# Two attention layers in one kernel: softmax sums out of the value products, division a step later, projections two steps ahead, and three of eight bias additions on GpSimd

## The reference

```
xn = layernorm(x)                                  # layer 0
s  = softmax(q k / sqrt(8) + bias[h]) v  @ w_out   # 16 heads of 8, bias from relative position
g  = silu(top-2-of-8 experts(xn))
x  = x + s * g
xn = layernorm(x)                                  # layer 1
a  = resid * softmax(causal(q k / sqrt(8))) + skip * eye - centre * uniform
x  = x + (a v @ cproj) * silu(xn W + xn V C + b)
```

## Time and profile before

| what | us |
|---|---|
| median of 3 runs | 1045.06 (1040.49 to 1049.14) |
| span of the profiled execution, first to last instruction | 1042.1 |
| setup, to the first projection | 0 to 76 |
| first layer's attention | 76 to 489 |
| experts and middle | 489 to 733 |
| second layer's attention | 733 to 1042 |

### The profile page before, as it was taken

The page is one execution under the profiler, slowest core; times in us unless marked ns, Lnnn a source line. Parts: engine busy times, 40 slices in busy tenths (PEclk is TensorE's granted clock), DMA queues, the critical chain, the costliest instruction groups (busy, mean ns, idle before and its releaser), DMA issues.

```text
span 1042.1 us, 22685 instructions
## 1 busy us (share of the span) xinstructions
PE 867.5 (83%) x7795; PEld 551.3 (53%) x7814; DVE 728.4 (70%) x1177; ACT 456.1 (44%) x808; POOL 393.3 (38%) x421
## 2 busy tenths in 40 slices
PE   1884887999999999987999998525689999999986
PEld 0742443555555555544555555314467667676763
DVE  5564686999899999985665555365456767676763
ACT  1251333545444554533433333258354445454532
POOL 7007772111111111100577776673134334344432
PEclk9996788999999999997999999856899999999998
DMA  4797441332223333204122122240544453435320
GB/s 135 232 142 173 111 113 44 82 75 62 62 63 74 76 81 72 61 7 140 37 59 53 54 56 56 69 125 16 118 98 89 98 103 97 103 97 103 97 44 11
DMA packets 105527, 88.21 MB, mean 85 GB/s; under 512 B 12565, under 2 KB 97497, under 8 KB 102409
## 3 DMA queue, kind: packets, MB, share of 16 engines
q1 hardware_dynamic: 96780, 76.54, 32.4%
q0 software_dynamic: 4352, 8.99, 2.8%
q10 hardware_dynamic: 4352, 2.10, 0.9%
HBM read 45.69 MB, written 41.11 MB: 83 GB/s over the span
## 4 chain that ended last, share of the span: by engine, by line
PE 19%; issue 14%; POOL 8%; DMA 5%; ACT 3%; DVE 3%; SPq 1%; POOLq 0%; ACTq 0%; DVEq 0%
PE ps L666 7%; POOL probs L1137 5%; PE ps L687 3%; DMA ks<-parts_d 3%; PE ps L678 2%; PE ps L660 2%; POOL qkr L1124 1%; ACT rows L888 1%; PE ps L668 1%; POOL qk L1129 1%; DMA parts_d<-qk 1%; PE ps L1469 1%; DVE mx L1191 1%; PE ps L1411 1%; DMA probs<-mixed 0%
## 5 line engine op out<-in xcount | busy, mean ns | idle before, releaser
L1191 DVE TENSOR_REDUCE mx<-ps 128x4 f32<-128x1024 f32 (+1 forms) x224 | 269.5, 1217 | 106.2 <-PE ps L1411 68.4
L1338 ACT ACTIVATE probs<-probs 128x1024 f32<-128x1024 f32 x128 | 135.3, 1057 | 165.6 <-DVE probs L1201 163.1
L1201 DVE TENSOR_TENSOR probs<-ps,tabB 128x1024 f32<-128x1024 f32 x128 | 152.4, 1212 | 3.6 <-PE ps L1431 3.6
L1343 ACT ACTIVATE probs<-ps 128x1024 f32<-128x1024 f32 x96 | 96.5, 1024 | 96.3 <-PE ps L1469 38.6
L1460 PE MATMUL ps<-probs,vpad 128*32 128x256 f32 (+1 forms) x2048 | 132.5, 365 | 3.0 <-ACT probs L1338 1.1
L1137 POOL TENSOR_TENSOR probs<-probs 128x512 f32<-128x512 f32 x64 | 78.9, 1264 | 136.7 <-PE ps L1460 136.7
L1403 PE MATMUL ps<-tabA,eyeb 128*128 128x512 bf16 x256 | 101.9, 398 | 31.2 <-DVE probs L1201 18.0
L1405 PE MATMUL ps<-ks,qs 96*128 96x256 bf16 x512 | 101.7, 281 | 0.0
L1431 PE MATMUL ps<-qs,ks 99*128 99x256 bf16 x512 | 76.7, 279 | 11.1 <-DVE mx L1191 6.0
L666 PE MATMUL ps<-qs,probs 128*128 x144 | 81.7, 650 | 1.4
L1460 PE MATMUL ps<-probs,onespad 128*32 128x256 f32 x1024 | 82.3, 394 | 0.0
(11 more groups left out here) (227 smaller groups left out, 1593.1 us busy)
## 6 DMA issues: line engine op xcount, KB each, us to landing
parts_d<-qk SPq DMA_DIRECT2D x64, 192.0 KB, 2.3
qs<-parts_d SPq DMA_DIRECT2D x32, 384.0 KB, 4.9
ks<-parts_d SPq DMA_DIRECT2D x32, 384.0 KB, 6.7
parts_d<-qk SPq DMA_DIRECT2D x64, 128.0 KB, 1.9
slots_in<-probs SPq DMA_DIRECT2D x1, 4680.0 KB
probs<-slots_in SPq DMA_DIRECT2D x72, 65.0 KB, 1.8
parts_d<-qk SPq DMA_DIRECT2D x64, 64.0 KB, 1.6
probs<-mixed SPq DMA_DIRECT2D x16, 256.0 KB, 3.3
```

The lines of the kernel that those rows point to most:

```text
L1191: nc.vector.tensor_reduce(mx[:, s.buf(), t, heads[0]:heads[-1] + 1], ring[:, slot].rearrange("p (h n) -> p h n", n=w), AX.X, ALU.max).then ...
L1201: nc.vector.tensor_tensor(probs[:, j, :].rearrange("p (h n) -> p h n", n=T), ring[:, slot].rearrange("p (h n) -> p h n", n=T), v.tabB[:, h ...
L1338: nc.scalar.activation(probs[:, j, :], probs[:, j, :], ACT.Exp).then_inc(exp_done, 1)
L1343: nc.scalar.activation(probs[:, j, :], ring[:, slot], ACT.Exp).then_inc(exp_done, 1)
```

## The change

What it does: (1) `vpad` gets eight columns of ones beside each head's eight values, so that one value product gives outputs and sums in one bank; `onespad`, the ones products, `sums` and `add_tiles` go. (2) `divide` goes. ScalarE copies the bank out, SP sends it to DRAM, reads the sums back as 128 by 32, VectorE inverts these, SP sends the inverses out and reads them back spread over eight partitions, and VectorE multiplies a step later (`scale`). Output projection, `add_shape`, `project` and store move from batch k-2 to k-3. (3) The projections and parts are for batch k+2 instead of k+1, and the stacks of k+1 are loaded at the start of SP's step. (4) In the first layer, from step 3 on, ScalarE copies B tiles 0, 2 and 4 out of PSUM (`take`), GpSimd adds their bias in place (`bias_aside`), and ScalarE takes their exponential two tiles later. The order of value products is changed to fit; the experts' weights are loaded from ScalarE's queue; the loop has three rounds and more steps are unrolled.

```diff
-        v.vpad = sb("vpad", [P, 3, 8, 160])
-        v.onespad = sb("onespad", [P, 4, 32])
+        v.vpad = sb("vpad", [P, 3, 8, 128])
+        v.od_d = nc.dram_tensor("od_d", (8, 2, 16, T), F32, kind="Internal")
+        v.rec_d = nc.dram_tensor("rec_d", (H, T), F32, kind="Internal")
...
+            nc.gpsimd.memset(v.vpad[:].rearrange("p b c (i w) -> p (b c i) w", w=32)[:, :, HD:2 * HD], 1.0
+                             ).then_inc(zeroed, 1)
...
-    LATE = 2 if layer else 6
-    PROJECT = 10 if layer else 11
-    LOOP = 3
+    LATE = 2 if layer else 4
+    SCALE = 2 if layer else 0
+    INVERT = 7 if layer else 10
+    VALUES = {9: (0, 1)} if layer else {13: (0, 1), 15: (2, 3)}
+    ASIDE = () if layer else (0, 2, 4)
+    ORDER = tuple(range(NU)) if layer else (1, 0, 3, 2, 5, 6, 4, 7)
+    PROJECT = 10 if layer else 8
+    LOOP, HELP = 4, 3
-    LAG = {"QK": 1, "V": 0, "E": -2, "Y": -2, "M": 0}
+    LAG = {"QK": 2, "V": 0, "E": -3, "Y": -3, "M": 0}
...
+            def parts(s, c):
+                b = s.buf(2)
+                (done,) = ahead(s.n(2) + 1)
+                sp.wait_ge((s1_done, s2_done, s3_done)[c], done)
+                for a in range(2):
+                    sp.dma_start(v.parts_d[b, a, PART_ROWS[a][c]].rearrange("r p t -> p r t"), ...).then_inc(part_st, 16)
+            def outputs_out(s):
...
+                sp.wait_ge(ev_done, done)
+                for r in range(2):
+                    sp.dma_start(v.od_d[:, r].rearrange("k d t -> k (d t)"), ev[:, r, :]).then_inc(od_st, 16)
+            def sums_in(s):
...
+                sp.wait_ge(od_st, stored)
+                sp.dma_start(rec[:], bass.AP(v.od_d, HD * T, [[16 * T, H], [2 * H, HD], [1, 2 * H]])).then_inc(sum_ld, 16)
+            def outputs_in(s):
...
+                sp.dma_start(raw[:], v.od_d[:].rearrange("k r d t -> (k r) d t")[:, 0:HD]).then_inc(raw_ld, 16)
+            def inverses_out(s):
...
+                sp.wait_ge(rd_done, done)
+                sp.dma_start(v.rec_d[:, :].rearrange("h (e t) -> (h e) t", e=HD), rec[:]).then_inc(rec_st, 16)
+            def inverses_in(s):
...
+                sp.wait_ge(rec_st, written)
+                sp.dma_start(rden[:], v.rec_d[:, :].unsqueeze(1).broadcast_to([H, HD, T])).then_inc(rec_ld, 16)
...
+            def body(s):          # SP; each under its own s.has(...)
+                stacks(s); parts(s, 0); outputs_out(s); parts(s, 1); sums_in(s); outputs_in(s)
+                parts(s, 2); inverses_out(s); inverses_in(s); maxima(s)
...
+        def bias_aside(pool, s, n, j):
+            pool.wait_ge(taken, len(ASIDE) * (s.n() - HELP) + n + 1)
+            p = probs[:, j, :].rearrange("p (h n) -> p h n", n=T)
+            nc.gpsimd.tensor_tensor(p, p, v.tabB[:, heads[0]:heads[0] + 4, off:off + T], ALU.add).then_inc(biased, 1)
...
             def body(s):          # GpSimd
-                if layer and s.has(-2):
-                    for g in range(GROUPS):
-                        add_tiles(pool, s, g)
+                for n, j in enumerate(apart(s.k)):
+                    if n == 1 and s.has(2):
+                        rest_two(pool, nc.gpsimd, s)
+                    if s.has(-1):
+                        bias_aside(pool, s, n, j)
...
-            def divide(s):
+            def invert(s):
+                dve.wait_ge(sum_ld, 16 * (s.n(-2) + 1))
+                nc.vector.reciprocal(rec[:], rec[:]).then_inc(rd_done, 1)
+            def scale(s):
+                dve.wait_ge(raw_ld, 16 * (s.n(-3) + 1))
+                dve.wait_ge(rec_ld, 16 * (s.n(-3) + 1))
+                nc.vector.tensor_tensor(on[:], raw[:], rden[:], ALU.mult).then_inc(on_done, 1)
...
+            def take(s, j, slot):
+                act.wait_ge(full["B"], NU * s.n(-1) + j + 1)
+                nc.scalar.activation(probs[:, j, :], ring[:, slot], ACT.Copy).then_inc(taken, 1)
+            def outputs(s):
+                act.wait_ge(pv_done, NU * (s.n(-2) + 1))
+                nc.scalar.activation(ev[:].rearrange("p r t -> p (r t)"), od, ACT.Copy).then_inc(ev_done, 1)
...
                 for pos, (kind, j) in enumerate(U.order):          # ScalarE
+                    if pos == (0 if layer else 4) and s.has(-2):
+                        outputs(s)
                     if kind == "B" and U.exists(s.k, kind):
-                        exponential(s, j, U.slot(s.k, pos))
+                        if j in apart(s.k):
+                            take(s, j, U.slot(s.k, pos))
+                        else:
+                            exponential(s, j, U.slot(s.k, pos))
+                        if apart(s.k) and j in (2, 4, 6):
+                            exponential(s, j - 2, 0)
...
-                for what in range(2 if layer == 0 else 1):
-                    for n, h in enumerate(heads):
-                        lhs = vpad[:, b, 4 * c + q, 32 * i:32 * i + 32] if what == 0 else onespad[:, i, :]
+                for n, h in enumerate(heads):
+                    at = 32 * i - 16 * (i // 2)
+                    mm = nc.tensor.matmul(od[32 * q:32 * q + 32, T * (i % 2) + t0:T * (i % 2) + T],
+                                          vpad[:, b, 4 * c + q, at:at + 32], probs[:, j, w * n:w * n + w], ...)
-            def sums(s, g):
...
                 for pos, (kind, j) in enumerate(U.order):          # TensorE
-                    if layer == 0 and pos == 1:
-                        last_values()
-                    if pos == 1 and s.has(1) and s.k != 0:
+                    if layer == 0 and pos in (1, 3):
+                        late_values(pos + 3, pos + 5)
+                    if pos == 1 and s.has(2):
                         projections(s)
```

More of the change, by code:

```diff
@@ L1056, in heads_of, with apart, freed, ready @@
         return range(8 * (j - 4), 8 * (j - 4) + 8), (0 if kind == "A" else 1), P
+    def apart(k):
+        return ASIDE if k >= HELP else ()
+    def freed(s, d, j):
+        m, aside = s.n(d), apart(s.k + d)
+        if not aside:
+            return used["B"], NU * (m - 1) + j + 1
+        if j in aside:
+            return taken, len(aside) * (m - HELP) + aside.index(j) + 1
+        before = sum(i not in aside for i in range(j))
+        return used["B"], NU * (HELP - 1) + (NU - len(aside)) * (m - HELP) + before + 1
+    def ready(s, d, j):
+        return NU * (s.n(d) - 1) + (ORDER.index(j) if apart(s.k + d) else j) + 1
     def emit(eng, body):
-        pipeline(eng, body, 0 if layer else -1, LOOP, 4, B + 1, 3, B)
+        pipeline(eng, body, -1 if layer else -2, LOOP, 3, B + 2, 3, B)
     with nc.Block() as block:
@@ L1070, in stacks @@
                 b = s.buf(1)
-                first, second, third, stored, scored = ahead(
-                    s.n(1) + 1, s.n(1) + 1, s.n(1) + 1, 16 * PART_DMAS * (s.turn(1) + 1), NU * (s.n(-2) + 1))
-                for c, made, wait in ((0, s1_done, first), (1, s2_done, second), (2, s3_done, third)):
-                    sp.wait_ge(made, wait)
-                    for a in range(2):
-                        rows = PART_ROWS[a][c]
-                        sp.dma_start(v.parts_d[b, a, rows].rearrange("r p t -> p r t"),
-                                     qk3[:, a, c, :].unsqueeze(1).broadcast_to([P, PARTS - c, T])
-                                     ).then_inc(part_st[b], 16)
-                sp.wait_ge(part_st[b], stored)
+                stored, scored = ahead(16 * PART_DMAS * (s.n(1) + 1), NU * (s.n(-2) + 1))
+                sp.wait_ge(part_st, stored)
                 if s.has(-2):
@@ L1097, in body @@
                     stacks(s)
+                if s.has(2):
+                    parts(s, 0)
+                if s.has(-2):
+                    outputs_out(s)
+                if s.has(2):
+                    parts(s, 1)
+                if s.has(-2):
+                    sums_in(s)
+                    outputs_in(s)
+                if s.has(2):
+                    parts(s, 2)
+                if s.has(-2):
+                    inverses_out(s)
+                    inverses_in(s)
                 if s.has():
@@ L1102, in _ @@
                 ahead_of[0](sp)
-                body(first)
+                for c in range(PARTS):
+                    parts(first, c)
                 sp.wait_ge(v.cleared, 4)
@@ L1264, in project @@
                     nc.vector.tensor_tensor(y, xt, y, ALU.add).then_inc(fin_done, 1)
             def body(s):
-                if layer == 0 and s.k == 0:
-                    rest_one(dve, nc.vector, s)
-                    rest_two(dve, nc.vector, s)
                 for pos, (kind, j) in enumerate(U.order):
-                    if layer == 0 and pos == 1 and s.has(-2):
-                        divide(s)
+                    if pos == SCALE and s.has(-3):
+                        scale(s)
                     if U.exists(s.k, kind):
-                        (maximum if kind == "A" else add_bias if layer == 0 else lambda *a: None)(s, j, U.slot(s.k, pos))
-                    if kind == "A" and j == NU - 1 and s.has() and (layer or s.k < LOOP):
```

(13 more changed lines are left out.)

219 lines of the change are left out of this document (113 added, 106 removed).

## The result

The changed kernel takes 1001.93 us (median; 998.65 to 1002.62) beside 1042.78 us of the kernel before in the same comparison: ratio 0.9584, 95% interval 0.9542 to 0.9626. Forecast 989, range 961 to 1030. Its profiled execution has a span of 999.9 us. ScalarE's copy of the transposed maxima marks the end of each step in both traces (106.18, 135.12, ... before; 110.43, 136.31, ...

What follows compares the result with a forecast made beforehand. VectorE was taken to bound the first layer's loop, TensorE the second's. First layer -7, -38, +5.5 and second -3, -15.5, +2 make -56 from 1042.1, to 986; the median 3.0 above gives 989, range 961 to 1030.

Steps and rivals of the forecast that it cites:

- First layer's step: First attention loop: a chain through last exponential, maxima's copy, projections and score tiles gives 19.9 us, 2.9 us less a step.
- Rival (b): First layer: GpSimd's additions take 4 us instead of 2.5, copies and exponentials queue behind, 1 us a step, 1002; chance 0.05.
- signs of being wrong: Reciprocals waiting for DMA in the first layer, low clock in the loops, ScalarE waiting for GpSimd.
- Start: First layer's start: 7 us less, from the 6.00 us scatter wait and 1 us of ones products on a slow clock.
- End of the first layer: Last exponential to last output: four landings of about 2 us, +7.5; the last step gives 2 back, +5.5 in all.
- Second layer's step: Second attention loop: SP's ordered transfers close the step before TensorE does, at 16.3 us, 1.2 us less a step.
- SP's chain: SP's ordered queue: stacks' loads, stores, outputs out, then sums in, for VectorE's reciprocal; sets second-layer steps at 16.3 us.
- Rival (a): Second layer isn't held by SP's queue and goes at TensorE's 15.1 us a step: another 15.5 less, 973; chance 0.12.
- The lock: VectorE's new product and GpSimd block each other in SBUF: 0.4 us a step at most, some 10 us in all.
- End of the second layer: The end grows from 12.7 us to about 16, +4, and the last step gives 2 back: +2.
- rival c: TensorE's clock falls in first-layer steps: half its path slow, 1024, chance 0.11; whole path slow, 1059, chance 0.03.
- rival d: SP's transfers from outputs out to sums in land later than priced; decides from 2.3 us extra, at 3.5 about 1080; chance 0.07.

Runs made afterwards that it cites:

- no_aside: Changed kernel with part 4 undone: VectorE adds all eight biases, ScalarE makes no copies, GpSimd adds none; 1017.58 us.
- rows_early: Changed kernel with ScalarE copying the first layer's transposed maxima out before its last exponential instead of after it; 994.25 us.
- take_first: Changed kernel with ScalarE copying first-layer tile 4 out for GpSimd before tile 3's exponential instead of after it; 998.12 us.
- all_edits: Changed kernel with both second-layer edits, earlier weights, earlier tile 4 and maxima copies, GpSimd's help from step 4, and tile 4's exponential before tiles 5 and 6; 964.85 us.
- weights_early: Changed kernel with the experts' weight loads issued behind tile 2's exponential in the first layer's last step instead of behind the last exponential; 995.13 us.
- scale_first: Changed kernel with the second layer's VectorE product of outputs and inverses moved to the start of the step; 995.07 us.
- both edits: Changed kernel with the second layer's product moved to the step's start and SP issuing the outputs' stores before the first part's stores; 988.00 us.
- parts_vector: Changed kernel with the first layer's maxima's parts made by VectorE behind its last maximum instead of by GpSimd; 1049.16 us.
- outputs_first: Changed kernel with SP issuing the second layer's two output stores ahead of the first part's two stores; 996.63 us.
- help_later: Changed kernel with GpSimd beginning to help in the first layer in step 4 instead of step 3; 996.14 us.

## Why the prediction was right, and which term was off

- **First layer's step: right.** 19.92 us over twelve steps (20.05 without the first and the last two), 19.9 forecast; the two idle stretches of VectorE are there, a third before tile 0 costs nothing in the sum. The same chain gave 21.3 for no_aside, measured 21.37. Its last link was too simple: the last exponential's copy, value tile 4 behind its exponential, and the parts behind GpSimd's third addition all reach the projections within about 0.5 us. Taking away one (rows_early, take_first) shows nearly nothing; the third had to go too (all_edits).
- **Parts' costs: right.** GpSimd's addition 2.37 us (2.5 taken), ScalarE's copies 1.01 and 0.59, reciprocal 0.35, product 0.41. The first layer's reciprocals wait for no DMA in a full step. Rival (b) is off. Of the forecast's signs of being wrong one came, in a single step: in step 3 ScalarE waits for GpSimd.
- **Start: near in the sum (-7.4 for -9.9) by luck.** "A step later the scattering is over" held for VectorE's output. The forecast left out that GpSimd itself, which part 4 needs in that very step, comes free no sooner. Steps 1 and 2 gained 13.5 us where 7 were forecast, step 3 lost 1.8 instead of gaining 2.9, and the setup lost 4.2, which lies within its spread.
- **End of the first layer: the mis-sized term, +13.7 for +5.5.** From the last exponential to the last output it was +15.0 for +7.5. The forecast put the weights "beside" this chain and priced its landings at 2 us; the first took 8.3, and in a steady step 3.9. weights_early shows that the weights did that, for 3.5 us against the changed kernel and 2.5 against the best run with the loads in their place. Of the rest, the last value products ran at almost half speed (3.58 us for 1.93, clock 0.53 for 1.00), after TensorE had stood 2.38 us. The last step's -2 was -1.3.
- **Second layer's step: near in size (16.55 for 16.3), half right in cause.** SP's chain exists and has the size forecast (16.42 in scale_first), but the reciprocal waited for it in few steps, since VectorE was as late by the product held up beside GpSimd. Rival (a), TensorE's 15.1, needs both limits away; with both edits 15.86 was reached.
- **The lock: cost wrongly bounded.** The forecast gave the rule of the Trainium skill (SBUF — State Buffer, section "Who interferes with whom") 0.4 us a step at most, the product's own length. By that rule, in my words, the one that comes second is blocked for the whole instruction of the other; the trace agrees: what counts is GpSimd's 1.16 us (product 1.29 for 0.48, second layer) or what was left of its 2.37 us (pass 1.98 for 0.18, parts_vector). In the first layer the product isn't held up (0.41 us). The price could be read before the change: in the middle part of the kernel before, a VectorE product of 128x512 took 1.73 us beside GpSimd's additions and 0.68 beside a GpSimd fill, and GpSimd's own addition 1.72 instead of 1.26. Timelines of VectorE and GpSimd before:

```profile
681.54 1.73 DVE L832 TENSOR_TENSOR probs<-probs,rows 128x512 f32<-128x512 f32 x1 [13.62 <-POOL probs L821]
...
691.18 0.68 DVE L832 TENSOR_TENSOR probs<-probs,rows 128x512 f32<-128x512 f32 x1
...
682.68 1.72 POOL L821 TENSOR_TENSOR probs<-probs 128x512 f32<-128x512 f32 x1
```

- **End of the second layer: -0.2 for +2.** From the last exponential (981.33) to the last result 16.3 us, +3.5 for +4; the last step gained 3.8 instead of 2. In the eight other runs with the second layer untouched this whole stretch takes 29.8 to 32.0 us, so 2 us can't be told here.
- **Clock (rival c): not in the changed kernel's loops (1.00).** One edit away it is there: in parts_vector TensorE waits 2.11 us in each step, and 1.4 us of slow products follow. With it the kernel is no faster than before.
- **Slower (rival d): off.** In the steps SP's chain never cost the extra 2.3 us from which it decides; only at the first layer's end did a landing take that much more.
- **The 13 us between 989 and 1001.93:** 8.2 are the first layer's end, 3.4 the second layer's thirteen steps, 2.5 the start with step 3, 2.2 the experts and the middle; the rest gives some 3.5 back.

## What to carry to other kernels

Some VectorE passes that work in SBUF alone (here a product of two SBUF tiles and a cast of 128x32) cost what is left of the GpSimd pass beside them, so look for a place in the step where GpSimd is idle before trusting their usual duration. Not all do: the bias additions, with one operand in PSUM, took 1.21 us beside GpSimd as without it. When no engine is full, list all chains that reach the late instruction and their slack: with three inside 0.5 us, an edit of one proves nothing against it, and edits are tried in pairs. A chain of small transfers at the end of a stage is to be priced with whatever large load is issued beside it.

## What the runs showed of the hardware that was not expected

One VectorE pass of the setup, over 128x16 elements in SBUF, took 0.18 us in one run (no_aside), 1.64 in the kernel before, 4.19 in the changed kernel and 4.71 at most (outputs_first), with the pass itself unchanged. In all fourteen profiles it ended within 0.03 us of the end of one of GpSimd's fills, which follow each other without a gap: at 9.54 us, 11.28, or 13.88 to 13.95. In the changed kernel it ended at 13.95, as the fill of `nothing` did at 13.92. So it was held up not only by the fill that it met but by up to three more behind it. When it starts doesn't decide how long: started at 9.24 it took 4.71 us in one run and 0.30 in another. The reduction of 128x2048 elements just ahead of it, also in SBUF and beside the fills, took 2.29 us in every run. Timelines of VectorE and GpSimd after, then of VectorE in outputs_first and in help_later:

```profile
7.43 2.29 DVE L564 TENSOR_REDUCE stat<-x 128x16 f32<-128x2048 f32 x1 [4.67 <-DMA x<-in_L_attn_x_dram]
9.76 4.19 DVE L566 TENSOR_SCALAR stat<-stat 128x16 f32<-128x16 f32 x1
...
11.19 2.67 POOL L408 MEMSET vpad<- 128x3072 f32 x1
13.79 0.13 POOL L409 MEMSET nothing<- 128x32 f32 x1
```
```profile
9.24 4.71 DVE L566 TENSOR_SCALAR stat<-stat 128x16 f32<-128x16 f32 x1
```
```profile
9.24 0.30 DVE L566 TENSOR_SCALAR stat<-stat 128x16 f32<-128x16 f32 x1
```

In the changed kernel's profile this pass cost 2.5 us that the kernel before didn't pay. The four profiles in which it ended last have the longest setups, 108.69 to 110.43 us; the nine others of this code have 105.76 to 108.66. Which fill lets it through, and why the rest of the setup's spread arises, stays open.
